# A split's low part on GpSimd: one 128x2048 subtraction in place of four of 128x512

## The reference, cut to what matters

```
x = x + softmax(layernorm(x) @ ctx.T) @ ctx        # cross attention, no scale
x = x + attention_over_heads(layernorm(x))         # small: Wq, Wk, Wv, biases
x = x + W_base and routed low-rank adapters on layernorm(x)
```

## Time and profile before

| | |
|---|---|
| median of 3 runs | 2553.24 us (2550.48 to 2562.08) |
| the profiled execution: its own time | 2560.45 us |
| the profiled execution: span | 2558.6 us |
| TensorE (PE) busy | 2458.9 us, 96% |
| VectorE (DVE) busy | 1975.5 us, 77% |
| ScalarE (ACT) busy | 1081.6 us, 42% |
| GpSimd (POOL) busy | 1265.1 us, 49% |
| mean granted TensorE clock | 0.969 of full |

### The profile page before, as it was taken

One profiled execution on the slowest core, in us unless ns is written; L12 is line 12 of the kernel. 1 busy time (PEld: TensorE's weight loads), 2 busy tenths in 40 slices (PEclk: granted clock), 3 DMA queues, 4 the chain that ended last, 5 costly groups with the idle time before them and its releaser, 6 DMA issues.

```text
span 2558.6 us, 35034 instructions
## 1 busy us (share of the span) xinstructions
PE 2458.9 (96%) x11342; PEld 2025.2 (79%) x11342; DVE 1975.5 (77%) x2668; ACT 1081.6 (42%) x1547; POOL 1265.1 (49%) x896
## 2 busy tenths in 40 slices
PE   6999999999999999999999999999999999894799
PEld 4888888888888888888888888888888888763677
DVE  7788888888888888888888887787878778532668
ACT  4444444444444444444444444444444444222323
POOL 4455556565556556655665565555555555410000
PEclk9999999999999999999999999999999999996579
DMA  9787887788788778878887877787777777667046
GB/s 243 200 217 182 215 202 195 200 209 212 194 206 213 195 196 209 206 197 213 201 204 194 210 190 189 191 196 184 192 184 186 188 188 192 166 138 113 5 85 145
DMA packets 377515, 476.14 MB, mean 186 GB/s; under 512 B 48707, under 2 KB 265795, under 8 KB 374853
## 3 DMA queue, kind: packets, MB, share of 16 engines
q1 hardware_dynamic: 373894, 454.68, 73.3%
q0 software_dynamic: 3584, 20.97, 2.6%
HBM read 467.74 MB, written 7.86 MB: 186 GB/s over the span
## 4 chain that ended last, share of the span: by engine, by line
PE 89%; DMA 4%; DVE 3%; SPq 2%; ACT 1%; POOL 1%; issue 1%; DVEq 0%; ACTq 0%
PE ps L1004 28%; PE ps L1006 28%; PE ps L1005 28%; PE ps L1013 2%; DMA raw<-in_L_attn_Wv_dram 1%; DMA q_t<-qk_dram 1%; DVE ch_lo L768 1%; PE ps L1034 1%; SPq L330 1%; DMA raw<-in_ctx_dram 1%; POOL nat_lo L475 1%; PE ps L1197 1%; DVE tr L764 1%; ACT nat_hi L557 1%; PE ps L1165 0%
## 5 line engine op out<-in xcount | busy, mean ns | idle before, releaser
L475 POOL TENSOR_TENSOR nat_lo<-raw,nat_hi 128x512 fp32r<-128x512 f32 x800 | 1172.8, 1496 | 933.3 <-ACT nat_hi L557 931.0
L768 DVE TENSOR_TENSOR ch_lo<-tr,ch_hi 128x512 fp32r<-128x512 f32 x848 | 949.9, 1120 | 362.6 <-ACT ch_hi L534 360.7
L534 ACT CAST ch_hi<-tr 128x512 fp32r<-128x512 f32 x848 | 517.2, 621 | 876.2 <-PE ps L1006 857.1
L1004 PE MATMUL ps<-ch_hi,xt_hi 128*128 128x512 f32 x1696 | 674.5, 398 | 8.1 <-DVE ch_lo L768 7.7
L1006 PE MATMUL ps<-ch_hi,xt_lo 128*128 128x512 f32 x1696 | 663.5, 391 | 0.0
L1005 PE MATMUL ps<-ch_lo,xt_hi 128*128 128x512 f32 x1696 | 662.9, 391 | 0.0
L1004 PE MATMUL ps<-nat_hi,pt_hi 128*128 128x512 f32 x1568 | 610.3, 389 | 2.9 <-DVE pt_lo L698 2.9
L1006 PE MATMUL ps<-nat_hi,pt_lo 128*128 128x512 f32 x1568 | 610.2, 389 | 0.0
L1005 PE MATMUL ps<-nat_lo,pt_hi 128*128 128x512 f32 x1568 | 610.0, 389 | 0.0
L764 DVE STREAM_TRANSPOSE tr<-quart 128x512 f32<-128x512 f32 x848 | 592.8, 699 | 3.9 <-DMA quart<-in_L_ffn_W_base_dram 3.8
L557 ACT CAST nat_hi<-raw 128x2048 fp32r<-128x2048 f32 x208 | 397.5, 1911 | 276.9 <-PE ps L1006 215.3
(11 more groups left out here) (126 smaller groups left out, 941.7 us busy)
## 6 DMA issues: line engine op xcount, KB each, us to landing
quart<-in_ctx_dram SPq DMA_DIRECT2D x392, 512.0 KB, 8.3
raw<-in_ctx_dram SPq DMA_DIRECT2D x196, 1024.0 KB, 7.8
wq_in<-in_L_attn_Wq_dram POOLq DMA_DIRECT2D x16, 1024.0 KB, 11.9
quart<-in_L_ffn_W_base_dram SPq DMA_DIRECT2D x32, 512.0 KB, 8.6
wq_dram<-wq_out POOLq DMA_DIRECT2D x16, 256.0 KB, 2.3
raw<-in_L_attn_Wk_dram SPq DMA_DIRECT2D x4, 1024.0 KB, 6.3
raw<-wq_dram SPq DMA_DIRECT2D x4, 1024.0 KB, 5.2
raw<-in_L_attn_Wv_dram SPq DMA_DIRECT2D x4, 1024.0 KB, 17.6
```

Source lines behind the costliest of these rows:

```text
L475: last = pool.tensor_tensor(nat_lo[:, j, t], raw[:, j % 2, t], nat_hi[:, j, t].bitcast(F32), ALU.subtract)
L534: act.copy(ch_hi[:, c % RING_CH, :], tr[:, c % RING_TR, :]).then_inc(chunk_hi, 1)
L768: dve.tensor_tensor(ch_lo[:, c % RING_CH, :], tr[:, c % RING_TR, :], ch_hi[:, c % RING_CH, :].bitcast(F32), ALU.subtract).then_inc(chunk_s ...
L1004: pe.matmul(out_, a_hi, b_hi, start=start, stop=False)
```

## The change

The four subtractions of a row tile each (128x512) in `lo_piece` become one subtraction over the whole piece (128x2048). The operands, the output and the semaphore are the same; `nat_ready[j]` is signalled by the one instruction as it was by the last of four.

```diff
--- before.py
+++ after.py
@@ -471,9 +471,7 @@
             def lo_piece(j, ready):
 
                 pool.wait_ge(nat_hi_ready, ready)
-                for t in range(KT):
-                    last = pool.tensor_tensor(nat_lo[:, j, t], raw[:, j % 2, t], nat_hi[:, j, t].bitcast(F32), ALU.subtract)
-                last.then_inc(nat_ready[j], 1)
+                pool.tensor_tensor(nat_lo[:, j], raw[:, j % 2], nat_hi[:, j].bitcast(F32), ALU.subtract).then_inc(nat_ready[j], 1)
 
             def split_block(turn):
                 for j in range(PIECES):
```

## The result

The changed kernel takes 2721.69 us (median of 4 runs, 2718.78 to 2725.59) against 2552.93 us before (4 runs). The ratio is 1.065, with a 95% interval of 1.0626 to 1.0674: 169 us slower. The forecast was 2668 us, 2595 to 2775.

A forecast was written before the change was run, and what follows sets the result against it. TensorE, busy for 96% of the span, was taken as the bound. Waits of 91 us, clock 19 and first block 6, less 1.5, made 114.5 us, giving 2668 us on 2553.24; range 2595 to 2775.

The forecast's parts named there:

- Removed: Three GpSimd instructions fewer per piece; worth only -1.5 us, from a few pieces at the end of the context loop.
- The length D: Duration of the merged GpSimd subtraction, during which VectorE's `ch_lo` is held; taken as 4.53 us.
- (a): Piece 1's subtraction holds VectorE's `ch_lo`, so the maxima on VectorE start 1.70 us late.
- (b): Softmax and piece 2 follow the late maxima; piece 2's hold then puts the second `pt_lo`'s end at 1807.73.
- the walk: Step-by-step timing of VectorE's instructions from piece 1's hold through piece 2's to TensorE's first piece product.
- (c): TensorE's first piece product waits for the second `pt_lo`, 1.94 us late in 47 periods: 91 us.
- (d): TensorE's clock falls behind such gaps, 1.64 us each time, taken for one in four: 19 us.
- (e): First block: two holds make VectorE some three chunks late for TensorE, 3 us twice: 6 us.
- SP's queue: Claimed unchanged: `nat_ready` comes at 4.53 instead of 5.95 us, so reloads are issued earlier, never later.
- The profile to expect: Line 475 about 200 instructions near 4.5 us, one `ch_lo` of 4.5 to 4.8 us per piece, about 47 `pt_lo` waits near 2 us.
- the third hold: Rival, chance 0.10: piece 3's hold gets ahead of chunk 7's `ch_lo`; TensorE waits 7.3 us a period, 2902 us.
- VectorE's slack: Rival, chance 0.08: VectorE's 1.25 us to spare at the second `pt_lo` hides the holds; not slower, 2555 us.

The follow-up runs named there:

- e2: Against the kernel before: only pieces 1 and 2 are subtracted in one instruction, pieces 0 and 3 in four; 2720.0 us, ratio 1.0615.
- e3: Against the kernel before: only pieces 0 and 3 are subtracted in one instruction, the others in four; 2560.1 us, ratio 1.0007.
- e4: The changed kernel with nine filler matmuls in front of TensorE's wait for `pt_lo`, their result overwritten; 2675.9 us, ratio 1.0466.
- e11: Against the kernel before: only the four pieces of the first block are subtracted in one instruction each; 2563.7 us, ratio 1.0028.
- e12: e8 with SP's reload of piece 0 issued ahead of the reload of the chunk buffer's first half; 2609.7 us, ratio 1.021.
- e8: e7 with ScalarE's cast of piece 3 one chunk later, behind chunk 8's cast; 2606.9 us, ratio 1.02.
- e7: The changed kernel with VectorE's second `pt_lo` moved ahead of chunk 7's `ch_lo`; 2628.9 us, ratio 1.028.
- e5: Against the kernel before: only piece 1 is subtracted in one instruction, the other pieces in four; 2591.3 us, ratio 1.0124.
- e9: The two order changes of e8, with pieces 1 and 2 in one instruction and 0 and 3 in four; 2610.6 us, ratio 1.0208.
- e6: The changed kernel with the subtraction left out but for eight columns, memsets that read nothing in its place; 2555.0 us, ratio 0.9988.
- e1: Against the kernel before: each piece is split into two subtractions of 128x1024; 2616.4 us, ratio 1.0227.

## Why the prediction was right, and where it was short

The direction, the mechanism and the place were right; the time was 54 us short of the measured one, inside the range. By its steps:

- **Removed.** The last pieces' gain of 1.5 us is too small to be seen.
- **The length D** was taken as 4.53 us, with bounds of 4.25 and 5.03. It is 4.61.
- **(a) and (b)** held to a tenth, with some luck: each hold was some 0.08 us longer than was taken, and the steps behind it were as much shorter in sum. The maxima were to be 1.70 us late against the piece's start and are 1.71 (8.76 - 7.05). The chain from piece 2 to the second `pt_lo` is 11.19 us long where the walk had 1807.04 - 1795.85 = 11.19.
- **(c)** was 1.94 us in 47 periods, 91 us. A period is 46.8 - 44.49 = 2.3 us longer, 108 us for 47; some 2.0 us of it are recorded as idle. The walk let TensorE start when `pt_lo` ends. In the trace its first matmul comes 0.25 us behind that end (1841.36 + 0.67 = 1842.03, 1842.28), and the one after it 0.34 us later in place of 0.23. This step was missing. That the recorded idle time agrees with 1.94 is no check of the walk: it counts from the end of the last matmul's record, which overlaps the next matmul by 0.16 us. e2 and e3 show that it is this chain and these two holds: in e2, with these two, the loss is whole, in e3, with the other two, it is nothing.
- **(d) was mis-sized.** The clock was taken as lost behind one wait in four, 19 us. It is lost behind 29 of 48, 46 us, and e4 shows that it comes from the gaps. The two gaps of before bounded it at 0 and 77 us, and the share between was a guess. The price of one loss, 1.64 us, held (1.6 measured).
- **(e)** was 6 us; e11 has 7.
- **SP's queue was misjudged.** The prediction had the reloads issued earlier, never later. SP issues in order, and the chunk reload waits for VectorE's eighth transposition of a period, which the holds delay; piece 0's reload stands behind it. The sums of SP's waits, before and after, 60 to 2150 us:

```profile
SPq L323 <- POOL nat_lo L475: 1125.2, 187, 11.1
SPq L330 <- DVE tr L764: 646.0, 94, 14.5
```

```profile
SPq L330 <- DVE tr L762: 1185.1, 88, 19.2
SPq L323 <- POOL nat_lo L474: 597.2, 101, 9.0
```

  In the changed kernel ScalarE waits only 10 us for `raw` in the loop, and undoing the order in e12 changed the time of e8 by nothing that could be measured; the step was wrong, and no run shows a price for it.
- **The profile to expect** was right for lines 474 and 696. That one `ch_lo` is held in each piece was wrong for piece 3, where `rescale`'s 128x2 multiplication takes the hold.

The terms as measured make 97 (100 less the 3 us that were there before) + 14 (48 x 0.3 not recorded as idle) + 46 + 7 = 164 us; the profiled spans differ by 2722.3 - 2558.6 = 163.7. Each term is known to a few us only, so the agreement is closer than it could be asked to be.

The rivals: the third hold missed by 0.51 us, the walk's own margin (chunk 7's `ch_lo` at 1839.51, the hold at 1840.02), and e7 shows what it does when it comes first. In the last period of the loop it came true, with D at 4.6: the third hold gets ahead of chunk 7's `ch_lo` by 0.54 us, and TensorE waits 7.53 us, where the rival had 7.3. VectorE has one more operation in front of the maxima there (line 851, 2.23 us); that this is why the hold gets ahead is read from the trace and not tried. GpSimd, VectorE and TensorE:

```profile
2320.18 4.50 POOL L474 TENSOR_TENSOR nat_lo<-raw,nat_hi 128x2048 fp32r<-128x2048 f32 x1 [4.19 <-ACT nat_hi L555]
```

```profile
2304.50 2.23 DVE L851 TENSOR_REDUCE wq_out<-wq_in 1x512 f32<-1x2048 f32 x1
...
2320.72 4.52 DVE L766 TENSOR_TENSOR ch_lo<-tr,ch_hi 128x512 fp32r<-128x512 f32 x1
...
2326.41 0.67 DVE L696 TENSOR_TENSOR pt_lo<-ps,pt_hi 128x512 fp32r<-128x512 f32 x1
```

```profile
2327.14 0.80 PE L1002 MATMUL ps<-nat_hi,pt_hi 128*128 128x512 f32 x1 [7.53 <-DVE pt_lo L696]
```

VectorE's slack does take holds at some places: e3 is that rival come true for pieces 0 and 3. It fails at piece 1: TensorE waits 0.3 us a period when that hold is alone (e5), and 2 us when piece 2's follows in the same chain. The hold at 1065 us was no single case either: the trace of before has 15 `ch_lo` of over 4 us beside four short subtractions run without a break, one in every second block up to 1421 us, and TensorE waited for none. So VectorE gets its turn at most boundaries between short instructions, but not at every one.

## What to carry to other kernels

An instruction that shares a resource with another engine by turns holds it for its whole length, so joining four into one saves their starts on an idle engine and lengthens the longest wait of a busy one. Ask of the longest wait where in the other engine's order it falls and how much that place has to spare; the sum of the waits, or the engine's idle time, doesn't tell (e3 against e2, e9).

## What the runs showed of the hardware

- GpSimd's subtraction of 128x2048 takes 4.61 us and four of 128x512 take 5.04, so an instruction that is saved is worth (5.04 - 4.61) / 3 = 0.14 us, on GpSimd alone.
- The turn-taking asks for two inputs in SBUF on VectorE (`pt_lo`, with one in PSUM, takes 0.67 us inside a hold) and reading on GpSimd: memsets of 3.5 us hold nothing (e6). A 128x2 multiplication is held as well, for 2.65 us. The Trainium skill, "SBUF — State Buffer", section "Who interferes with whom", states both sides of this; the traces agree. That the first to issue has the shared ports for its whole instruction it says of another case, VectorE's 2-port mode; here the traces show it for two inputs (4.69 us of `ch_lo` beside 4.61).
- TensorE at the 2.4 GHz level, busy for 45 us, loses the level behind 29 of 48 waits, nearly all of 2.0 us, and that costs nearly half as much again as the waits (46 us on 100). Behind the waits of some 0.8 us in e1 the granted clock stays at 1.00. Why 19 of the waits kept the level is not shown.
